# New prologue, V projection ahead of the next heads, first queries' shares on ScalarE

## The reference

```python
# cond(r, k, v): per channel a decayed sum over earlier and later positions
ek  = exp(min(k, 30)); ekv = ek * v                  # k = v = fside
nf, df = forward scan of ekv, ek with decay; nb, db = the same backward
euk = exp(min(u + k, 30))
num = nf + nb - ekv + euk * v; den = df + db - ek + euk
cond = sigmoid(r) * num / max(den, 1e-8) * (0.8 + 0.2 * tf)
# attention: 16 heads of 128, causal
q, k, v = W_Q y, W_K y, W_V y;  z = softmax(mask(q k)) v;  out = W_O z
# ffn: 8 experts, two best by gate, softmax over the two
x = x + attention(cond(x, f, f, w, u));  x = x + ffn(cond(x, f, f, w2, u2))
```

## Time and profile before

| what | value |
|---|---|
| median of 3 runs | 388.52 us (388.48 to 388.64) |
| profiled execution | 388.69 us, span 386.8 us |
| busy PE, DVE | 357.1 us (92%), 315.2 us (81%) |
| busy ACT, POOL | 219.7 us (57%), 210.1 us (54%) |
| mean granted clock | 0.994 |

### The profile page before, as it was taken

How to read it: one execution, slowest core, us unless ns; L and a number is a source line. 1 busy time by engine, 2 the same in 40 slices (tenths; PEclk the granted TensorE clock), 3 DMA queues, 4 the chain that set the end, 5 groups by cost and what they waited for, 6 DMA issues and landing times.

```text
span 386.8 us, 7608 instructions
## 1 busy us (share of the span) xinstructions
PE 357.1 (92%) x2534; PEld 332.8 (86%) x2534; DVE 315.2 (81%) x883; ACT 219.7 (57%) x616; POOL 210.1 (54%) x231
## 2 busy tenths in 40 slices
PE   0578888999999999999999999999999998999996
PEld 0467878999999899999999999999999987877885
DVE  3979988897889788988988898889757694676675
ACT  3648567648655766775667576665666463221000
POOL 3677977645553567956865776677554333110000
PEclk9999899999999999999999999999999999999999
DMA  6651050010000000031100004100000000000000
GB/s 219 217 170 50 0 164 2 19 39 1 2 0 2 1 3 2 11 110 47 53 3 2 1 20 146 56 2 1 3 0 2 2 1 3 0 14 14 28 29 27
DMA packets 4598, 14.14 MB, mean 37 GB/s; under 512 B 840, under 2 KB 1872, under 8 KB 3920
## 3 DMA queue, kind: packets, MB, share of 16 engines
q1 hardware_dynamic: 4416, 13.65, 10.6%
q10 hardware_dynamic: 144, 0.00, 0.0%
HBM read 12.60 MB, written 1.05 MB: 35 GB/s over the span
## 4 chain that ended last, share of the span: by engine, by line
PE 81%; DVE 10%; issue 2%; POOL 2%; ACT 2%; DMA 1%; SPq 0%; DVEq 0%; ACTq 0%; POOLq 0%
PE psQK L850 9%; PE psQK L852 9%; PE psQK L851 9%; PE psT L910 5%; PE psZ L850 4%; PE psO L852 4%; PE psO L850 4%; PE psO L851 4%; PE psS L901 4%; PE psS L850 4%; PE psZ L852 4%; PE psZ L851 4%; PE psS L851 4%; PE psS L852 4%; PE psV L850 4%; PE psV L852 3%
## 5 line engine op out<-in xcount | busy, mean ns | idle before, releaser
L472 ACT ACTIVATE prob<-prob,ntop 128x256 f32<-128x256 f32 (+1 forms) x128 | 57.3, 449 | 93.3 <-DVE ntop L690 93.3
L301 POOL TENSOR_SCALAR prob<-prob,rsum 128x128 f32<-128x128 f32 x64 | 38.9, 607 | 104.7 <-DVE rsum L698 104.7
L850 PE MATMUL psQK<-y_hi,w_hi 128*128 128x256 f32 x256 | 73.3, 286 | 1.3 <-DVE y_lo L613 1.1
L852 PE MATMUL psQK<-y_hi,w_lo 128*128 128x256 f32 x256 | 73.0, 285 | 0.0
L851 PE MATMUL psQK<-y_lo,w_hi 128*128 128x256 f32 x256 | 72.9, 285 | 0.0
L302 POOL TENSOR_SCALAR prob<-prob,rsum 128x256 f32<-128x256 f32 x64 | 59.8, 935 | 0.0
L266 POOL TENSOR_TENSOR w_lo<-raw,w_hi 128x512 fp32r<-128x512 f32 x40 | 52.9, 1334 | 6.6 <-ACT w_hi L356 6.4
L850 PEld LDWEIGHTS psQK<-y_hi,w_hi 128*128 128x128 f32 x256 | 49.3, 193 | 2.2 <-DVE y_lo L613 1.3
L852 PEld LDWEIGHTS psQK<-y_hi,w_lo 128*128 128x128 f32 x256 | 49.3, 193 | 0.0
L851 PEld LDWEIGHTS psQK<-y_lo,w_hi 128*128 128x128 f32 x256 | 49.3, 193 | 0.0
L702 DVE TENSOR_TENSOR qk<-psQK,qk 128x512 fp32r<-128x512 f32 x64 | 43.6, 682 | 6.5 <-ACT qk L460 4.8
(11 more groups left out here) (176 smaller groups left out, 1044.3 us busy)
## 6 DMA issues: line engine op xcount, KB each, us to landing
raw<-in_weights SPq DMA_DIRECT2D x5, 1024.0 KB, 6.5
raw<-in_weights SPq DMA_DIRECT2D x10, 512.0 KB, 4.2
out<-fT SPq DMA_DIRECT2D x8, 128.0 KB, 2.0
fT<-in_fT SPq DMA_DIRECT2D x2, 256.0 KB, 6.5
xT<-in_xT SPq DMA_DIRECT2D x2, 256.0 KB, 8.4
fT<-in_fT SPq DMA_DIRECT2D x1, 512.0 KB, 10.2
xT<-in_xT SPq DMA_DIRECT2D x1, 512.0 KB, 10.9
wu<-in_wu ACTq DMA_DIRECT2D x1, 4.0 KB, 1.6
```

Of the source, the lines that this page charges most:

```text
L301: pool.tensor_scalar(prob[:, k, 0:P], prob[:, k, 0:P], rsum[:, k, 0:1], None, ALU.mult)
L472: ins = act.activation(prob[:, k, lo:hi], prob[:, k, lo:hi], ACT.Exp, scale=-1.0, bias=ntop[:, k, q:q + 1], accum_out=ssum[:, k, q:q + 1])
L850: pe.matmul(out, ah, bh, start=first and k == 0, stop=False)
L852: ins = pe.matmul(out, al, bh, start=False, stop=last and k == n - 1)
```

## The change

Prologue: temb is loaded from ACT's queue; SP waits for fT before it issues the weights; POOL's three products are gone, ekv and eukv are made on DVE into psum banks; ACT makes three exponentials less; DVE's order changes; WARM is 5. Units: the V projection comes right after the scores (the very first one ahead of unit 0), `v_high` after `exps`, `v_low` after `reciprocals` in the same unit. Shares: ACT multiplies the first 128 columns in every unit and the others too in units 2 and 3. Clamps and exponentials of later sequences come one unit earlier, some weight copies move from E to M, and the order at the end changes.

```diff
-DVE_PLACES = {"min": (-2, "E"), "xd": (0, "M"), "xn": (1, "M"), "gd": (2, "M"), "gn": (3, "M"), "den": (4, "M"),
+DVE_PLACES = {"min": (-3, "E"), "xd": (0, "M"), "xn": (1, "M"), "gd": (2, "M"), "gn": (3, "M"), "den": (4, "M"),
...
-ACT_PLACES = {"exps": (-1, "E"), "sxd": (0, "E"), "sxn": (1, "E"), "e1": (2, "E"), "yhi": (7, "E")}
+ACT_PLACES = {"exps": (-2, "E"), "sxd": (0, "E"), "sxn": (1, "E"), "e1": (2, "E"), "yhi": (7, "E")}
...
+SHARES_ACT = (2, 3)
-WARM = 7
+WARM = 5
...
-    f_ek, f_euk = halves(psQK[0]), halves(psS[0])
+    f_ek, f_ekv, f_euk, f_eukv = (halves(bank) for bank in (psQK[0], psQK[1], psS[0], psT))
-    f_e1, f_eukv = t0[:, XD], t0[:, XN]
+    f_e1 = t0[:, XD]
...
@@  SP
-        sp.dma_start(temb[:], ap["temb"]).then_inc(in_temb, 16)
         load_f(0, 1, in_f0)
+        sp.wait_ge(in_f0, 16)
         load_qk(0)
...
@@  POOL
             pool.wait_ge(recipd, u + 1)
-            pool.tensor_scalar(prob[:, k, 0:P], prob[:, k, 0:P], rsum[:, k, 0:1], None, ALU.mult)
             pool.tensor_scalar(prob[:, k, P:3 * P], prob[:, k, P:3 * P], rsum[:, k, 1:2], None, ALU.mult).then_inc(shared, 1)
...
-        pool.wait_ge(f_act, 2)
-        pool.tensor_tensor(t0[:, EKV], t0[:, EK], cols(fT, 0), ALU.mult).then_inc(f_pool, 1)
-        pool.wait_ge(f_act, 4)
-        pool.tensor_scalar(t0[:, EUK], t0[:, EUK], EXP_LIMIT, None, ALU.min).then_inc(f_pool, 1)
-        pool.wait_ge(f_pool, 2)
-        pool.tensor_tensor(f_eukv, t0[:, EUK], cols(fT, 0), ALU.mult).then_inc(f_pool, 1)
...
-            shares(u)
+            if u not in SHARES_ACT:
+                shares(u)
...
@@  ACT
+        act.dma_start(temb[:], ap["temb"]).then_inc(in_temb, 16)
         act.dma_start(wu[:], ap["wu"]).then_inc(in_wu, 16)
...
         act.activation(f_ek, t0[:, EK], ACT.Exp).then_inc(f_act, 1)
-        act.activation(t0[:, EK], t0[:, EK], ACT.Exp).then_inc(f_act, 1)
-        for c in range(CB):
-            act.activation(t0[:, EUK, c], fT[:, 0, c], ACT.Exp, bias=wu[:, 1, c:c + 1]).then_inc(f_act, 1)
+        for c in range(CB):
+            act.activation(f_euk[:, c], fT[:, 0, c], ACT.Exp, bias=wu[:, 1, c:c + 1]).then_inc(f_act, 1)
...
+        def shares(u):
+            k = u % 2
+            act.wait_ge(recipd, u + 1)
+            act.activation(prob[:, k, 0:P], prob[:, k, 0:P], ACT.Copy, scale=rsum[:, k, 0:1]).then_inc(first_shared, 1)
+            if u in SHARES_ACT:
+                act.activation(prob[:, k, P:3 * P], prob[:, k, P:3 * P], ACT.Copy, scale=rsum[:, k, 1:2]).then_inc(shared, 1)
...
-                at(u, "E", refill, kind, g, part)
+                at(u, "M" if u % GH < TT and g > 1 else "E", refill, kind, g, part)
...
-        at(63, "M", gates_copy, 0)
+        at(62, "E", gates_copy, 0)
...
         qk_high(1)
+        v_high(0, 0)
         cond(1)["exps"]()
         for u in range(UNITS):
             exps(u)
+            if h < TT and u:
+                v_high(i, h)
             do(u, "M")
             if u + 2 < UNITS:
                 qk_high(u + 2)
             if 2 <= u:
                 z_high(u - 2)
+            shares(u)
             if 1 <= u:
                 pT_high(u - 1)
             do(u, "E")
-            if h < TT:
-                v_high(i, h)
         z_high(UNITS - 2)
+        pT_high(UNITS - 1)
         tanh(2)
-        pT_high(UNITS - 1)
...
@@  DVE, prologue
+        dve.tensor_tensor(f_ekv, f_ek, cols(fT, 0), ALU.mult).then_inc(f_dve, 1)
...
+        dve.wait_ge(f_dve, 4)
+        for c in range(CB):
+            forward(f_xn[c], f_ekv[:, c], 0, c, 0).then_inc(f_dve, 1)
+        for c in range(CB):
+            dve.wait_ge(f_act, 4 + c)
+            backward(t0[:, GD, c], f_xd[c], 0, c, 0).then_inc(f_dve, 1)
+        dve.wait_ge(f_act, 3)
+        dve.scalar_tensor_tensor(f_eukv, f_euk, EXP_LIMIT, cols(fT, 0), ALU.min, ALU.mult).then_inc(f_dve, 1)
+        for c in range(CB):
+            dve.wait_ge(f_act, 6 + c)
+            backward(t0[:, GN, c], f_xn[c], 0, c, 0).then_inc(f_dve, 1)
+        for c in range(CB):
+            dve.wait_ge(f_dve, 7 + c)
+            dve.scalar_tensor_tensor(f_xd[c], f_euk[:, c], EXP_LIMIT, t0[:, GD, c], ALU.min, ALU.add).then_inc(f_dve, 1)
...
-        dve.wait_ge(f_act, 12)
+        dve.wait_ge(f_act, 9)
...
-        dve.wait_ge(f_pool, 3)
...
@@  DVE, units
-            if 1 <= u:
-                i, h = (u - 1) // GH, (u - 1) % GH
-                if h < TT:
-                    v_low(i, h)
             maxima(u)
             do(u, "M")
             reciprocals(u)
+            i, h = u // GH, u % GH
+            if h < TT:
+                v_low(i, h)
...
+        y2_last(3)
         gate_last(2)
-        y2_last(3)
         add_experts(6)
         add_experts(7)
+        add_experts(8)
         gate_first(3)
-        add_experts(8)
+        add_experts(9)
         gate_last(3)
...
@@  PE
             pe.wait_ge(shared, u + 1)
+            pe.wait_ge(first_shared, u + 1)
...
-        pe.wait_ge(f_dve, 6)
+        pe.wait_ge(f_dve, 7)
...
+        project_v(0, 0)
         for u in range(UNITS):
             scores(u)
+            if h < TT and u:
+                project_v(i, h)
...
-            if u == UNITS - 1:
-                gates_turn(1)
-            if h < TT:
-                project_v(i, h)
-            elif i:
+            if h >= TT and i:
                 output(i - 1, h - TT)
...
             if u == UNITS - 1:
+                gates_turn(1)
                 base(0)
...
-        late = {7: [(logits, 3)], 9: [(gates_turn, 2)], 10: [(base, 2)], 11: [(gates_turn, 3)], 12: [(base, 3)]}
+        late = {8: [(logits, 3)], 9: [(gates_turn, 2)], 10: [(base, 2)], 12: [(gates_turn, 3)], 13: [(base, 3)]}
```

More of the change, by code:

```diff
@@ L155, in build @@
     pre_dve, pre_act = sem("pre_dve"), sem("pre_act")
-    f_dve, f_act, f_pool = sem("f_dve"), sem("f_act"), sem("f_pool")
+    f_dve, f_act = sem("f_dve"), sem("f_act")
     c_dve, c_act, c_pool = ([sem(f"c_{n}{k}") for k in range(2)] for n in ("dve", "act", "pool"))
@@ L163, in build @@
     scored, masked, maxed, exped, recipd, shared = (sem(n) for n in ("scored", "masked", "maxed", "exped", "recipd", "shared"))
+    first_shared = sem("first_shared")
     turned, pT_hi_done, pT_ready = sem("turned"), sem("pT_hi_done"), sem("pT_ready")
@@ L379, in _ @@
         for c in range(CB):
-            act.activation(f_euk[:, c], fT[:, 0, c], ACT.Exp, bias=wu[:, 1, c:c + 1]).then_inc(f_act, 1)
-        for c in range(CB):
-            act.wait_ge(f_dve, 4 + c)
+            act.wait_ge(f_dve, 5 + c)
             scaled(f_xn[c], 0, c, 0).then_inc(f_act, 1)
@@ L385, in _ @@
         act.activation(f_e1, cols(xT, 0), ACT.Exp, scale=-1.0).then_inc(f_act, 1)
-        act.wait_ge(f_act, 11)
+        act.wait_ge(f_act, 8)
         act.activation(f_e1, f_e1, ACT.Copy, bias=1.0).then_inc(f_act, 1)
@@ L516, in _ @@
         for c in range(CB):
-            act.wait_ge(f_dve, 16 + 4 * c)
+            act.wait_ge(f_dve, 18 + 4 * c)
             act.activation(y_hi[:, 0, c], f_xn[c], ACT.Copy).then_inc(f_act, 1)
@@ L533, in _ @@
             do(u, "E")
-            i, h = u // GH, u % GH
-            if h < TT:
-                v_high(i, h)
         z_high(UNITS - 2)
+        pT_high(UNITS - 1)
         tanh(2)
-        pT_high(UNITS - 1)
         z_high(UNITS - 1)
@@ L585, in _ @@
         dve.scalar_tensor_tensor(rest[:], decay[:], 1.0, rest[:], ALU.add, ALU.mult).then_inc(pre_dve, 1)
+        dve.wait_ge(f_dve, 4)
[9 more added lines that the diff above has]
+            backward(t0[:, GN, c], f_xn[c], 0, c, 0).then_inc(f_dve, 1)
         dve.tensor_scalar(tout[:], tf[:], 0.2, 0.8, ALU.mult, ALU.add).then_inc(pre_dve, 1)
+        for c in range(CB):
+            dve.wait_ge(f_dve, 7 + c)
+            dve.scalar_tensor_tensor(f_xd[c], f_euk[:, c], EXP_LIMIT, t0[:, GD, c], ALU.min, ALU.add).then_inc(f_dve, 1)
         dve.wait_ge(pre_dve, 10)
         dve.tensor_scalar(thalf[:], tout[:], 0.5, None, ALU.mult).then_inc(pre_dve, 1)
-        dve.wait_ge(f_pool, 1)
+        dve.wait_ge(f_act, 9)
         for c in range(CB):
-            forward(f_xn[c], t0[:, EKV, c], 0, c, 0).then_inc(f_dve, 1)
-        for c in range(CB):
-            dve.wait_ge(f_act, 5 + c)
-            backward(t0[:, GD, c], f_xd[c], 0, c, 0).then_inc(f_dve, 1)
-        for c in range(CB):
-            dve.wait_ge(f_act, 9 + c)
-            backward(t0[:, GN, c], f_xn[c], 0, c, 0).then_inc(f_dve, 1)
-        for c in range(CB):
-            dve.wait_ge(f_dve, 6 + c)
-            dve.scalar_tensor_tensor(f_xd[c], f_euk[:, c], EXP_LIMIT, t0[:, GD, c], ALU.min, ALU.add).then_inc(f_dve, 1)
-        dve.wait_ge(f_act, 12)
-        for c in range(CB):
-            dve.wait_ge(f_dve, 10 + c)
+            dve.wait_ge(f_dve, 12 + c)
             dve.scalar_tensor_tensor(f_xd[c], f_xd[c], 1e-8, f_e1[:, c], ALU.max, ALU.mult).then_inc(f_dve, 1)
@@ L607, in first_y @@
             dve.tensor_tensor(f_xn[c], f_eukv[:, c], t0[:, GN, c], ALU.add).then_inc(f_dve, 1)
```

(26 more changed lines are left out.)

## The result

The changed kernel takes 383.97 us in the median of four runs (382.85 to 386.08), the kernel before 388.5 in the same series: ratio 0.989 (0.9873 to 0.9906), 4.5 us less where 12.2 were forecast. It is faster by 1.1%, clear of the noise, but 7.5 us slower than predicted and outside the range. The profiled execution is the slowest of the four, 386.08 us with a span of 384.1, and the one in which the clock fell most: the mean granted clocks of the four are 0.985 (386.08 us), 0.990 (384.63), 0.995 (382.85) and 0.999 (383.31).

What follows compares the result with a forecast made beforehand. The prediction took TensorE to bound the long middle and DVE to pace the ramp. Start -5.2, ramp -1.3, middle -3.0 and end -2.7 summed to -12.2 from 388.7, giving 376.5 us, range 373.0 to 381.0.

Steps and rivals of the forecast that it cites:

- Shares: First 128 columns moved from GpSimd to ACT in each unit: costed at nothing, up to 0.2 us a unit without cover.
- the sign that the prediction named: Wrong if: clamp after 5, psZ wait in each V block, clock 0.50 before 60, or pT_low idle for ACT mid-kernel.
- Rival 5: V units: ACT's wait for the reciprocal holds up pT_high beyond its 0.9 us slack; 390.9 us, chance 0.03.
- Landing of fT: Prologue: fT issued 0.6 us earlier, load taking 2.7 us, landing at 3.4 (2.6 to 5.6), 2.8 earlier.
- temb and wu: Prologue loads: their chain ends at about 3.6 and can hold up fT's by 0.2 us.
- tout and thalf: Prologue: the tout pair adds 0.25 us between the first backward scan and the reciprocal.
- additions of line 607: Prologue: two DVE additions, 1.11 and 1.50 us before, costed at 0.42 each with eukv in psum.
- Warm-up: Prologue: ends near 15 to 16, some 2 us idle before the first half projection; full clock, otherwise up to 1.5 us.
- Ramp: Last y_low to unit 8: 0.85 for later exponentials, less 1.7 DVE idle and 0.5 GpSimd relief: -1.3 us.
- rival 2: Ramp gives back as V projections wait for the previous v_low, and fT lands late: 380.3 us, chance 0.2.
- Middle: Waits ahead of values vanish with v_low in its projection's unit; 0.7 us late turn over 16 blocks: -3.0 us.
- End: Waits before psZ (0.72, plus 0.27 restart), a gates transpose (1.1) and the last logits (0.67) go: -2.7 us.

Runs made afterwards that it cites:

- e10: Changed kernel with tout and thalf early, WARM 6, and temb issued by SyncE between fT and the wait: 381.68 us, ratio 0.9829.
- e6: e4 with tout and thalf issued ahead of the scans, behind rest: 384.47 us, ratio 0.9882.
- e4: Changed kernel with a longer warm-up, WARM 8 in place of 5: 383.02 us, ratio 0.9864.
- e7: e4 with the second sequence's three exponentials ahead of v_high(0, 0) on ACT: 382.06 us, ratio 0.9835.
- e15: Changed kernel with tout and thalf early, WARM 6, second sequence's exponentials ahead of v_high(0, 0), gate_last(0) in unit 61, all shares on GpSimd: 378.23 us.
- e13: Kernel before with only the moved places of clamps, exponentials, weight copies and the order at the end: 385.52 us, ratio 0.9919.
- e8: e4 with gate_last(0) in unit 61 instead of 60 on DVE: 382.56 us, ratio 0.9844.
- e1: Kernel before with the new V order, including the gates' transpose of unit 63 behind its output projection: 386.51 us, ratio 0.9938.
- e5: e4 with all shares back on GpSimd: 383.24 us, ratio 0.9871.

## Why the prediction was wrong, point by point

**Shares, the step that failed.** "I cost it at nothing": alone they cost 3.9 us, in the combined version 2.0, the largest single piece of the 7.5. The cover that I named, DVE's reciprocal and two subtractions, is real for `pT_high` alone. I did not follow the rest of ACT's queue: what stands behind the share (scaled copies, `v_high`, the next exponentials) is late by 0.4 too, and in the units with scans DVE needs them at once. DVE's waits for `pT_high` went from one of 0.5 to 16 with 3.2 us in all. This was the sign that the prediction named as one that would make it wrong. Rival 5 named the mechanism and its side (slower), but priced it as all or nothing. Two more of its signs came: the clock at 0.50 before 60, and steps of over 5.2 after unit 8.

**Landing of fT.** Priced 2.7 us, took 3.2 (0.72 to 3.93): 0.5 of the miss. Within its bounds.

**temb and wu.** "Their chain can hold up fT's by 0.2": they are used from 4.20 and 4.26, and the first scan starts 2.09 us after the clamp instead of 1.35. That is 0.74 more, and `e10` shows that no order of the queues cures it.

**tout and thalf.** Priced 0.25, took 1.24 + 0.66 = 1.9. With `e6`'s place they take 0.16 each. Beside them in the slow place GpSimd was subtracting weights, as it was beside the additions of line 607. The same reading that I applied to the additions should have been applied to the operations that I moved. These three sum to 2.9; the start is 2.55 short of its forecast, since the stretch from the product ekv to the first backward scan took 2.44 and not 2.7. The additions came as forecast at 0.40 and 0.42. The row of 0.42 by which they were priced (24.09) had no subtraction of GpSimd beside it, and in the changed kernel only the first has; `e6` has both beside one, and they take 0.41 and 0.42.

**Warm-up.** "I take full clock, and up to 1.5 us for the other case": it was the other case. The idle time was 3.25 us, not 2: the warm-up, started at 10.45 and not 9.0, ended at 17.03, but the half projection waited until 20.28 and not 17.6. `e4` against the changed kernel puts the fall at 1.3. The run at 0.999 cannot have had it, as a fall of 3.4 us takes 0.004 off the mean; that run left no trace, so whether its idle time was the same is not known.

**Ramp.** +2.1 instead of -1.3. 1.3 of it is the fall of the clock above, which the four lines of the table put here. Without it (`e4`) the ramp is at +0.8. The delay of the first head's exponentials, priced 0.85, is worth 1.0 by `e7`. What failed is the gain of 1.7 + 0.5: DVE is not relieved, it is busy 34.06 us instead of 33.48, and the shares of units 2 and 3 on ACT cost 0.6 (`e15`) where they were to help. That is nearest to rival 2, which I gave 0.2: its V projections that wait for the previous `v_low` are there, 3.4 us of them. With exponentials and shares moved back (`e15`) unit 8 starts 42.15 us after the last `y_low`, 1.3 less than before, the size of the forecast without the relief of GpSimd that it counted on.

**Middle.** -2.75 against -3.0, the one large term that held, but not by the account given. Units 30, 38 and 46 fell to 4.59. Units 14 and 22 stayed at 5.33, since `pT_low` (not `v_low`) is the last to come. It ends at 96.84, with PE ready at 96.40:

```profile
96.30 0.54 DVE L718 TENSOR_TENSOR pT<-psT,pT 128x384 fp32r<-128x384 f32 x1
```

And I gave the moved copies and clamps "no price", while `e13` shows 1.95 us for them in this stretch alone.

**End.** +0.6 against -2.7. From unit 63 on 1.6 us were gained. The two waits for gates and logits, 1.77 together, are gone, but a new one of 0.9 ahead of a gates' transpose came in, so the other half of this gain is not traced. The rest of the forecast was "0.72 before psZ is gone": it became 1.33. `gate_last(0)` holds DVE until 310.40 in unit 61, `maxima` and `v_low` follow, and `pT_low` is late by as much. `e8` moved it, and part of the wait moved with it. The V order alone (`e1`) had already brought 1.10 there. In the profiled execution the clock fell after that wait, another 1.5 (8.61 against 7.08 for unit 62).

Taken back one by one, from the changed kernel's median of 383.97: the warm-up (`e4`) 1.0, tout early 1.5, the exponentials and the gate together 1.3, the shares 2.0. That is 5.7 of the 7.5 us and leads to the 378.23 of `e15`, inside the predicted range but 1.7 over its middle. Not cured in it are the 0.5 of fT, the 0.7 of the late decays and the wait of 0.9 at the end.

## What to carry to other kernels

Work moved to an engine with idle time is not free if the engine runs its queue in order: follow every instruction behind the new one to whoever waits for it in that unit, and try the move alone before it is mixed with others. Price a small operation by the row of the same size beside the same neighbours, not by its size. When a prologue is shortened, set the warm-up anew so that it ends where the first real product starts.

## What the runs showed of the hardware

- A 128x4 TENSOR_SCALAR on DVE took 1.24 us beside GpSimd's subtraction of weights (0.90 in `e4`) and 0.16 earlier in the prologue, with GpSimd idle (`e6`). In both slow cases it ended 0.03 us after the subtraction that was under way when it began. That GpSimd is the whole cause is not shown: in the kernel before the same operation took 0.16 in the middle of a GpSimd instruction. Additions with one operand in psum beside the same subtractions took 0.41 and 0.42 (`e6`) and were not lengthened.
- Two small loads (1 and 4 KB) issued at 0.7 to 1.3 took 2.9 to 3.3 us while the load of fT was under way, from either queue; issued ahead of it, in the kernel before, 1.9 and 1.6.
- In the profiled execution of the changed kernel the granted clock fell to 0.50 for 3.4 us after 3.25 us of idle time of PE. After waits of 1.3 to 1.8 us it fell in some executions and not in others of nearly the same kernel: at 31.6 and 314.9 in the changed kernel, at neither place in `e4` with waits of 1.82 and 1.33. With a wait of 2.7 us it fell in the profiled execution of `e5` (at 45.4, 0.2 before the wait's end) and not in that of `e15`. What decides this was not settled. The upper part of the spread of the changed kernel's runs (382.85 at 0.995 to 386.08 at 0.985) goes with it, but the run at 0.999 took 383.31, so it is not all.
